# A time-mix block on one core: four result tiles in place of two, and six sequences laid out as four successive tokens a partition

## The chip, the core and the metric

The kernel runs on one core of one Trainium2 chip. The metric is the device time of one execution in microseconds. Three runs of the kernel before gave 110.7, 111.28 and 111.68 us, a median of 111.28 us.

## The reference, cut to what matters

The input `x` holds 8 sequences of 512 tokens with 128 channels, in float32. Everything is computed per token, save a recurrence along the tokens of a sequence.

```python
xn = layernorm(x)                                    # over the 128 channels
shifted = xn one token later                         # zero for the first token
k = (xn*mk + shifted*(1-mk)) @ Wk                    # v and r likewise, r through a sigmoid
rwkv = scan over tokens(time_decay, time_first, k, v)  # needs the tokens in order
s = (r * rwkv) @ Wo
h = relu(xn @ w1[0] + b1[0]);  eo = h @ w2[0] + b2[0]  # 128 -> 512 -> 128, expert 0 alone counts
g = silu(layernorm(xn + eo) * gamma + beta)
return x + s * g
```

## The kernel before, in words

A sequence `b` is one unit of work. Its 512 tokens are loaded as rows: `x_sb` holds, for each partition `p`, four blocks `j` of 128 channels. In the kernel before block `j` of partition `p` is token `j*128 + p`, so a partition's four tokens lie 128 tokens apart in memory, and a transfer moves 512 bytes at a time. Everything per row (the statistics of the layer norm, the normalised tile `xn`) works on these blocks. Then TensorE transposes the four 128x128 blocks of `xn` into one bank of PSUM (step `T`, L613), so that the partitions are channels and the 512 columns are the tokens in order. `xn` is the stationary operand there and the identity the moving one, and block `j` goes to columns `j*128` to `j*128+127`. ScalarE copies the bank to `xT` (L497). From there everything runs on tiles of 128 channels by 512 tokens: the mixed inputs `ink`, `inv`, `inr` (L786), the projections `k`, `v`, `r` (L630), the up projections `up0` to `up3` with their operand split into two float32r parts (L651 to L653), the down projections `z0` to `z3`, which accumulate onto the bank that `T` wrote (L680), the variance `var` (L668), the recurrence by three scans on VectorE, the gate, and the output projection `s` (L661). At the end `prod` = `s` times `g` is transposed back to rows (step `back`, L689: `prod` is stationary, block `j` is its columns `j*128` to `j*128+127`), VectorE adds the input rows and writes a tile `res` (step `res`, L875), and SyncE's queue stores it (L309).

Work on the eight sequences is interleaved. `PROGRAM` is a hand-written order of steps for each engine: `res:5` is step `res` of sequence 5, and `res.a:7` is the first half of it. Each step waits on semaphores for what it reads, and for the release of the buffer that it writes. Nearly every tile exists twice, and step `b` waits for the reader of step `b - 2`. Sequences 0 and 7 are worked in halves at the start and at the end: sequence 0's rows come in two transfers of 128 KB, sequence 7's results leave in two, `a` on SyncE's queue and `b` on ScalarE's.

With two result tiles, `res:b` waits until the store of sequence `b - 2` has landed (`stored`, L872). The queue of SyncE holds in this order: half of `x` of sequence 0, `w1`, the four square weights, `x` of sequence 1, `w2`, `x` of sequences 2 to 7, the stores of sequences 0 to 6, and `store.a:7`.

The end of VectorE's order is `res:3 prod:5 gated:7 res:4 zn.b:7 zn.a:7 prod:6 res:5 prod.a:7 prod.b:7 res:6 res.a:7 res.b:7`, that of TensorE's `back:3 s:5 var.b:7 var.a:7 back:4 s:6 s.b:7 back:5 s.a:7 back:6 back.a:7 back.b:7`.

Of the kernel before, what the change touches and what calls it, by code (L numbers as in the profile page):

```python
# [7 lines left out]
ALU = mybir.AluOpType  # L8
# [4 lines left out]
WARM_UP = 8  # L13
KEEP_WARM_BETWEEN = 1
KEEP_WARM = 4
LN_EXP_TABLES = "natural_log_exp_and_others"
SILU_TABLES = "silu_and_others"

# [110 lines left out]
def build_block(nc, x, vectors, squares, w1, w2, out):  # L129
    B, T, H = x.shape  # L130
    P = 128
    NT = T // P
# [1 line left out]
    NF = F // P  # L134
    assert H == P and T == 512 and NT * P == T and NF * P == F

    x_rows = x.rearrange("b (j p) c -> b p j c", p=P)
    out_rows = out.rearrange("b (j p) c -> b p j c", p=P)
    HALVES = [slice(0, NT // 2), slice(NT // 2, NT)]

    B1_COLUMN = len(VECTORS)
# [5 lines left out]
    with ExitStack() as ctx:  # L147
        def sb(name, *shape, dt=FP32):
            return ctx.enter_context(nc.sbuf_tensor(name, list(shape), dt))

        def pair(name, *shape, dt=FP32):
            return [sb(f"{name}_{n}", *shape, dt=dt) for n in range(2)]


        ident = sb("ident", P, P)
# [22 lines left out]
        ve1 = sb("ve1", P, B * NT)  # L178
        rstd1 = sb("rstd1", P, B * NT)
        xn = pair("xn", P, NT, P)  # L180
        res = pair("res", P, NT, P)


        xT = pair("xT", P, 1 + T)
# [26 lines left out]
        prod = pair("prod", P, T)  # L211
# [3 lines left out]
        def ps(name, b, half=""):  # L215
            return banks[bank_of[name, half if (name, half, b) in bank_of else "", b]]

        def sem(name):
            return ctx.enter_context(nc.semaphore(name))
# [5 lines left out]
                 "w2_sum", "w2_mean", "w2"]}  # L225
        done = {(engine, name): sem(f"{name}_by_{engine}")
                for engine, name in dict.fromkeys((signal[token][0], token[0]) for token in signal if token[2] is not None)}
        stored = [sem(f"stored_{n}") for n in range(2)]
        EDGES = 11
        LAST = B - 1  # L230
        CHUNKS = [f"z{f}" for f in range(NF)]

        def after(eng, step, b, half=""):
            if b < 0 or (b == 0 and step in NOT_FOR_FIRST):
                return
            if (step, half, b) in signal:
                engine, count = signal[step, half, b]
            elif half:
                engine, count = signal[step, "", b]
            else:  # L240
                engine, count = max(signal[step, h, b] for h in "ab")
            eng.wait_ge(done[engine, step], count)
# [4 lines left out]
        def bank_free(eng, name, b, half=""):  # L247

            previous = held_before[name, half, b]
            if previous == ("b2m", "", None):  # L250
                eng.wait_ge(prep["cols"], 4)
            elif previous:
                for step in FREED_BY[previous[0]]:
                    after(eng, step, previous[2], previous[1])

        def chunks_of(b):

            return [name for name, _, i in tokens("pe") if name in CHUNKS and i == b]
# [4 lines left out]
        def tiles(half):  # L263
            return {"": slice(0, NT), "a": HALVES[0], "b": HALVES[1]}[half]
# [8 lines left out]
        def first_on(engine, step):  # L273
            return [b for name, _, b in tokens(engine) if name == step][0]
# [23 lines left out]
        def load_half(eng, h):  # L298
            tiles = HALVES[h]
            eng.dma_start(x_sb[:, tiles.start * P:tiles.stop * P].rearrange("p (j c) -> p j c", c=P),  # L300
                          x_rows[0][:, tiles, :]).then_inc(got[f"x0_{h}"], 16)

        def load(eng, b):
            eng.dma_start(x_sb[:, b * T:(b + 1) * T].rearrange("p (j c) -> p j c", c=P),
                          x_rows[b]).then_inc(got[f"x{b}"], 16)

        def store(eng, b, half=""):
            after(eng, "res", b, half)
            eng.dma_start(out_rows[b][:, tiles(half), :], res[b % 2][:, tiles(half), :]).then_inc(stored[b % 2], 16)  # L309

        block = ctx.enter_context(nc.Block())

        @block.sync
        def _(sp):
            load_half(sp, 0)
            sp.dma_start(w1_in[:, :], w1).then_inc(got["w1"], 16)
            sp.dma_start(w_in[:, :, :], squares).then_inc(got["squares"], 16)
            load(sp, 1)
            sp.dma_start(w2_in[:, :, :], w2.rearrange("(f p) c -> p f c", p=P)).then_inc(got["w2"], 16)
            for b in range(2, B):  # L320
                load(sp, b)
            for b in range(LAST):
                store(sp, b)
            store(sp, LAST, "a")
            sp.wait_ge(stored[0], 16 * (B // 2))
            sp.wait_ge(stored[1], 16 * (B // 2 + 1))

        @block.gpsimd
        def _(pool):
# [117 lines left out]
        def _(act):  # L447
# [3 lines left out]
            def ln_exp_tables():  # L451
                act.preload_act_table_set(LN_EXP_TABLES)  # L452

# [137 lines left out]
            steps.update({f"hid{f}": hidden(f) for f in range(NF)})  # L591
            run("act", steps)
            store(act, LAST, "b")

        @block.tensor
        def _(pe):
            def keep_warm(count):
                for _ in range(count):
                    pe.matmul(banks[WARM_BANK][:, 0:P], ident[:, :], ident[:, :], start=True, stop=True)  # L599
# [8 lines left out]
            def transposes(b, half=""):  # L608
                if half != "b":
                    bank_free(pe, "z", b)  # L610
                after(pe, "norm1", b, half)
                for j in range(NT)[tiles(half)]:
                    ins = pe.matmul(ps("z", b)[:, j * P:(j + 1) * P], xn[b % 2][:, j, :], ident[:, :], start=j == 0,  # L613
                                    stop=False, is_transpose=True, skip_group_check=True)
                ins.then_inc(done["pe", "T"], 1)
                if half == "a":
                    keep_warm(KEEP_WARM_BETWEEN)
                elif b == 0:
                    keep_warm(KEEP_WARM)

# [63 lines left out]
            def back_to_rows(b, half=""):  # L684
                after(pe, "prod", b, half)
                bank_free(pe, "back", b, half)
                rows = ps("back", b, half)[:, :].rearrange("p (j c) -> p j c", c=P)
                for j in range(NT)[tiles(half)]:
                    ins = pe.transpose(rows[:, j, :], prod[b % 2][:, j * P:(j + 1) * P], ident[:, :])  # L689
                ins.then_inc(done["pe", "back"], 1)  # L690

            pe.wait_ge(prep["ident"], 1)
            keep_warm(WARM_UP)
            steps = {"b2m": b2_mean, "T": transposes, "var": variance, "s": project_out, "back": back_to_rows}
            steps.update({name: projection(name) for name in "kvr"})
            steps.update({f"up{f}": up(f) for f in range(NF)})
# [4 lines left out]
        def _(dve):  # L701
# [166 lines left out]
            def add_input(b, half=""):  # L868
                t = tiles(half)
                after(dve, "back", b, half)  # L870
                if b >= 2:
                    dve.wait_ge(stored[b % 2], 16 * (b // 2))  # L872
                rows = x_sb[:, b * T:(b + 1) * T].rearrange("p (j c) -> p j c", c=P)
                summed = ps("back", b, half)[:, :].rearrange("p (j c) -> p j c", c=P)
                dve.tensor_tensor(res[b % 2][:, t, :], summed[:, t, :], rows[:, t, :], ALU.add).then_inc(done["dve", "res"], 1)  # L875

            steps = {"bn": stats, "aggr1": aggregate, "norm1": normalise, "d": step_of_x, "xT_lo": low_part, "dv": value_steps,
                     "cols": small_columns, "w2_sum": w2_row_sums, "mx": running_max, "gap": exponents,
                     "den": denominator, "rel": relative, "dev": deviation,
                     "wkv": mixed_values, "gated": gate, "zn": scale, "prod": multiply, "res": add_input,  # L880
                     "adev": weighted}
            steps.update({"in" + name: mix(name) for name in "kvr"})
# [35 lines left out]
```

## Time and profile before

| | before |
|---|---|
| median of three runs | 111.28 us |
| the profiled execution | 111.6 us |
| its span, first to last instruction | 109.8 us |
| TensorE busy | 100.7 us, 92% |
| VectorE busy | 99.3 us, 90% |
| ScalarE busy | 93.4 us, 85% |
| GpSimd busy | 67.0 us, 61% |
| mean granted clock of TensorE | 0.986 |

The span leaves out 1.8 us of the profiled execution. Three engines are busy for 85% and more of the span, so which of them sets the pace at a given place is read from the chain of waits, followed back from the last instruction, and from the table of busy times by stretch. A matmul's busy time overlaps that of the next; the time that a matmul adds is read from the chain, where each piece counts once.

### The profile page before, as it was taken

To read this page: it belongs to the slowest core of one execution; us is meant where nothing else is said; L and a number is where in the kernel's file an instruction comes from. 1 tells how busy PE (TensorE), PEld (TensorE's weight loads), DVE (VectorE), ACT (ScalarE), POOL (GpSimd) and SP (SyncE) were. 2 spreads that over 40 slices of the span, in tenths; PEclk is the share of its full clock that TensorE was granted. 3 is DMA by queue.
4 is the path that set the end of the run, shared out by engine and by line. 5 is a ranking of instruction groups with operands and counts; after the bars stand their busy time and mean duration, and the time that the engine had idled before them with its cause. 6 is when DMAs were issued, how large, how long until landed. Compare 5 with 4: busy or idle time off the path is not lost.

```text
span 109.8 us, 1625 instructions
## 1 busy us (share of the span) xinstructions
PE 100.7 (92%) x340; PEld 57.8 (53%) x340; DVE 99.3 (90%) x204; ACT 93.4 (85%) x155; POOL 67.0 (61%) x102
## 2 busy tenths in 40 slices
PE   4999989999699999999999999999989999999720
PEld 4998546654346465436574554754424565435410
DVE  1789799999889999998999899999999999999941
ACT  3550888999979999999999999999998999998800
POOL 3059699986838599999699669594645033700000
PEclk9999999999999999999999999999999999999995
DMA  2999300000000000000005000000000020001463
GB/s 90 279 314 291 83 0 0 0 6 0 3 0 3 0 0 0 0 0 0 0 15 178 1 6 0 0 0 3 0 0 0 0 96 0 9 0 57 134 191 99
DMA packets 9450, 5.09 MB, mean 46 GB/s; under 512 B 480, under 2 KB 9184, under 8 KB 9440
## 3 DMA queue, kind: packets, MB, share of 16 engines
q1 hardware_dynamic: 8752, 4.72, 15.3%
q10 hardware_dynamic: 688, 0.27, 0.9%
q14 instruction: 7, 0.06, 0.2%
q8 instruction: 3, 0.05, 0.2%
HBM read 2.89 MB, written 2.10 MB: 45 GB/s over the span
## 4 chain that ended last, share of the span: by engine, by line
PE 56%; issue 15%; POOL 13%; ACT 6%; DVE 5%; DMA 2%; DVEq 1%; POOLq 0%; ACTq 0%
PE bank L630 11%; PE bank L680 10%; PE bank L599 5%; PE bank L661 5%; PE bank L668 5%; PE bank L651 4%; POOL xn L359 4%; PE bank L653 4%; PE bank L652 4%; PE bank L613 3%; PE bank L643 3%; POOL xT_lo L381 2%; DMA block_out<-res 2%; POOL gap_max L415 2%; PE bank L689 2%
## 5 line engine op out<-in xcount | busy, mean ns | idle before, releaser
L680 PE MATMUL bank<-hid,w_c 128*128 128x512 f32 x64 | 30.8, 593 | 0.3 <-ACT hid L514 0.3
L630 PE MATMUL bank<-mixed,w_in 128*128 128x512 f32 x48 | 24.0, 599 | 1.1 <-POOL mixed L399 1.1
L514 ACT ACTIVATE hid<-bank,vec 128x512 f32<-128x512 f32 x28 | 18.8, 684 | 3.6 <-PE bank L643 2.9
L680 PEld LDWEIGHTS bank<-hid,w_c 128*128 128x128 f32 x64 | 11.9, 189 | 12.6 <-issue 11.6
L786 DVE SCALAR_TENSOR_TENSOR mixed<-step_x,vec,bank 128x511 f32<-128x511 f32 x24 | 17.2, 735 | 0.8 <-POOL step_x L390 0.8
L651 PE MATMUL bank<-xT_hi,w_hi 128*128 128x512 f32 x28 | 15.7, 560 | 0.0
L359 POOL TENSOR_SCALAR xn<-x_sb,neg_mean,rstd 128x128 f32<-128x128 f32 x28 | 14.1, 521 | 0.1
L630 PEld LDWEIGHTS bank<-mixed,w_in 128*128 128x128 f32 x48 | 8.4, 189 | 9.3 <-issue 8.2
L423 POOL TENSOR_TENSOR dv<-v_sb 128x512 f32<-128x512 f32 x8 | 8.9, 1108 | 6.1 <-ACT v_sb L567 6.1
L825 DVE TENSOR_TENSOR_SCAN dev<-keep,dv 128x512 f32<-128x512 f32 x8 | 11.5, 1435 | 0.6 <-issue 0.3
L653 PE MATMUL bank<-xT_lo,w_hi 128*128 128x512 f32 x28 | 11.1, 395 | 0.0
L652 PE MATMUL bank<-xT_hi,w_lo 128*128 128x512 f32 x28 | 11.0, 394 | 0.0
L795 DVE TENSOR_TENSOR_SCAN mx<-td,bank 128x512 f32<-128x512 f32 x8 | 9.7, 1210 | 0.7 <-PE bank L630 0.7
L430 POOL TENSOR_SCALAR keep<-th_g 128x512 f32<-128x512 f32 x8 | 5.8, 723 | 6.3 <-ACT th_g L573 6.2
L810 DVE TENSOR_TENSOR_SCAN den<-e_keep,bank 128x512 f32<-128x512 f32 x8 | 9.6, 1208 | 0.0
L452 ACT ACT_TABLE_LOAD x6 | 7.7, 1283 | 1.9 <-issue 1.8
L710 DVE BATCH_NORM_STATS2 stats<-x_sb 128x6 f32<-128x128 f32 x32 | 6.9, 278 | 2.6 <-DMA x_sb<-x 2.6
L381 POOL TENSOR_TENSOR xT_lo<-xT,xT_hi 128x512 fp32r<-128x512 f32 x7 | 8.9, 1267 | 0.3
L668 PE MATMUL bank<-sq,averager 128*128 128x512 f32 (+1 forms) x18 | 8.3, 557 | 0.5 <-DVE adev L833 0.5
L661 PE MATMUL bank<-gated,wo_half 128*128 128x512 f32 (+1 forms) x18 | 8.3, 553 | 0.0
L651 PEld LDWEIGHTS bank<-xT_hi,w_hi 128*128 128x128 f32 x28 | 5.3, 188 | 5.5 <-issue 2.1
L407 POOL TENSOR_SCALAR gap_min<-gap,td 128x512 f32<-128x512 f32 x8 | 5.5, 688 | 4.2 <-DVE gap L803 4.0
(72 smaller groups left out, 209.9 us busy)
## 6 DMA issues: line engine op xcount, KB each, us to landing
x_sb<-x SPq DMA_DIRECT2D x7, 256.0 KB, 5.4
block_out<-res SPq DMA_DIRECT2D x7, 256.0 KB, 2.3
w_in<-w SPq DMA_DIRECT2D x2, 256.0 KB, 4.0
w_in<-squares SPq DMA_DIRECT2D x1, 256.0 KB, 3.9
x_sb<-x ACTq DMA_DIRECT2D x1, 128.0 KB, 2.8
x_sb<-x SPq DMA_DIRECT2D x1, 128.0 KB, 2.5
block_out<-res SPq DMA_DIRECT2D x1, 128.0 KB, 1.9
block_out<-res ACTq DMA_DIRECT2D x1, 128.0 KB, 2.0
```

The lines of the kernel that those rows point to most:

```text
L359: ins = pool.tensor_scalar(xn[n][:, j, :], x_tile(b, j), neg_mean1[:, i:i + 1], rstd1[:, i:i + 1], ALU.add, ALU.mult)
L381: pool.tensor_tensor(xT_lo[n][:, :], xT[n][:, 1:], xT_hi[n][:, :].bitcast(FP32), ALU.subtract).then_inc(done["pool", "xT_lo"], 1)
L514: act.activation(hid[b % 2][:, f, :], ps(f"up{f}", b)[:, :], ACT.Relu, bias=vec[:, B1_COLUMN + f:B1_COLUMN + f + 1]).then_inc(done["act", ...
L630: pe.matmul(ps(name, b)[:, :], w_in[:, which, :], mixed[b % 2][:, which, :], start=True, stop=True).then_inc(done["pe", name], 1)
L651: pe.matmul(dst, hi, xT_hi[n][:, :], start=True, stop=False)
L652: pe.matmul(dst, lo, xT_hi[n][:, :], start=False, stop=False)
L653: pe.matmul(dst, hi, xT_lo[n][:, :], start=False, stop=True).then_inc(done["pe", f"up{f}"], 1)
L661: pe.matmul(ps("s", b, half)[:, c], wo_half[:, :], gated[b % 2][:, c], start=True, stop=True).then_inc(done["pe", "s"], 1)
L668: pe.matmul(ps("var", b, half)[:, c], averager[:, :], sq[b % 2][:, c], start=True, stop=True).then_inc(done["pe", "var"], 1)
L680: pe.matmul(ps("z", b)[:, :], w2_c[:, f, :], hid[b % 2][:, f, :], start=False, stop=chunks_of(b)[-1] == f"z{f}", skip_group_check=True).th ...
L786: dve.scalar_tensor_tensor(mixed[n][:, which, 1:], step_x[n][:, 1:], vec[:, which:which + 1], ps("z", b)[:, 0:T - 1], ALU.mult, ALU.add).t ...
L825: dve.tensor_tensor_scan(dev[n][:, :], keep[n][:, 0:T], dv[n][:, :], 0.0, ALU.mult, ALU.add).then_inc(done["dve", "dev"], 1)
```

## The change

Two things change.

The result tile `res` exists four times (`RES = 4`), each with its own semaphore. `res:b` waits for the store of sequence `b - 4`, and SyncE waits at the end for four semaphores in place of two.

For sequences 1 to 6 partition `p` holds tokens `4p` to `4p+3` instead of `p`, `p+128`, `p+256`, `p+384`. A partition's four rows are then 2048 successive bytes in memory, for the load and for the store. So that the channel tiles still hold the tokens in order, `T` writes block `j` into every fourth column of the bank, from column `j` on, and `back` reads every fourth column of `prod` as its stationary operand. Sequences 0 and 7, worked in halves, keep the old layout. The number of transposes, their shapes and the bytes moved stay as they are.

```diff
+RES = 4
-    x_rows = x.rearrange("b (j p) c -> b p j c", p=P)
-    out_rows = out.rearrange("b (j p) c -> b p j c", p=P)
+    IN_HALVES = [0, B - 1]
+
+    def rows_of_tokens(a):
+        tiled, woven = a.rearrange("b (j p) c -> b p j c", p=P), a.rearrange("b (p j) c -> b p j c", j=NT)
+        return [tiled[b] if b in IN_HALVES else woven[b] for b in range(B)]
+
+    def columns_of(b, j):
+        return slice(j * P, (j + 1) * P) if b in IN_HALVES else slice(j, T, NT)
+
+    x_rows = rows_of_tokens(x)
+    out_rows = rows_of_tokens(out)
...
-        res = pair("res", P, NT, P)
+        res = [sb(f"res_{n}", P, NT, P) for n in range(RES)]
...
-        stored = [sem(f"stored_{n}") for n in range(2)]
+        stored = [sem(f"stored_{n}") for n in range(RES)]
...
-            eng.dma_start(out_rows[b][:, tiles(half), :], res[b % 2][:, tiles(half), :]).then_inc(stored[b % 2], 16)
+            eng.dma_start(out_rows[b][:, tiles(half), :], res[b % RES][:, tiles(half), :]).then_inc(stored[b % RES], 16)
...
-            sp.wait_ge(stored[0], 16 * (B // 2))
-            sp.wait_ge(stored[1], 16 * (B // 2 + 1))
+            for n in range(RES):
+                sp.wait_ge(stored[n], 16 * (B // RES + (n == LAST % RES)))
...
-                    ins = pe.matmul(ps("z", b)[:, j * P:(j + 1) * P], xn[b % 2][:, j, :], ident[:, :], start=j == 0,
+                    ins = pe.matmul(ps("z", b)[:, columns_of(b, j)], xn[b % 2][:, j, :], ident[:, :], start=j == 0,
                                     stop=False, is_transpose=True, skip_group_check=True)
...
-                    ins = pe.transpose(rows[:, j, :], prod[b % 2][:, j * P:(j + 1) * P], ident[:, :])
+                    ins = pe.transpose(rows[:, j, :], prod[b % 2][:, columns_of(b, j)], ident[:, :])
...
-                if b >= 2:
-                    dve.wait_ge(stored[b % 2], 16 * (b // 2))
+                if b >= RES:
+                    dve.wait_ge(stored[b % RES], 16 * (b // RES))
...
-                dve.tensor_tensor(res[b % 2][:, t, :], summed[:, t, :], rows[:, t, :], ALU.add).then_inc(done["dve", "res"], 1)
+                dve.tensor_tensor(res[b % RES][:, t, :], summed[:, t, :], rows[:, t, :], ALU.add).then_inc(done["dve", "res"], 1)
```

No instruction moves on any engine. What a step waits for changes at one place, VectorE's last steps, with the semaphores that each waits for (`stored_1` is that of result tile 1). Of the kernel before:

```order
L875 TENSOR_TENSOR res<-bank,x_sb 128x512 [waits stored_0,back_by_pe]
L858 SCALAR_TENSOR_TENSOR zn<-bank,cb,rstd_1 128x256 [waits silu_by_act,rstd2_by_act,sq_by_act] x2
L866 TENSOR_TENSOR prod<-bank,g 128x512 [waits back_by_pe,s_by_pe,silu_by_act]
L875 TENSOR_TENSOR res<-bank,x_sb 128x512 [waits stored_1,back_by_pe]
L866 TENSOR_TENSOR prod<-bank,g 128x256 [waits back_by_pe,s_by_pe,silu_by_act] x2
L875 TENSOR_TENSOR res<-bank,x_sb 128x512 [waits stored_0,back_by_pe]
L875 TENSOR_TENSOR res<-bank,x_sb 128x256 [waits stored_1,back_by_pe] x2
```

The same steps after the change:

```order
L885 TENSOR_TENSOR res<-bank,x_sb 128x512 [waits stored_0,back_by_pe]
L868 SCALAR_TENSOR_TENSOR zn<-bank,cb,rstd_1 128x256 [waits silu_by_act,rstd2_by_act,sq_by_act] x2
L876 TENSOR_TENSOR prod<-bank,g 128x512 [waits back_by_pe,s_by_pe,silu_by_act]
L885 TENSOR_TENSOR res<-bank,x_sb 128x512 [waits stored_1,back_by_pe]
L876 TENSOR_TENSOR prod<-bank,g 128x256 [waits back_by_pe,s_by_pe,silu_by_act] x2
L885 TENSOR_TENSOR res<-bank,x_sb 128x512 [waits stored_2,back_by_pe]
L885 TENSOR_TENSOR res<-bank,x_sb 128x256 [waits stored_3,back_by_pe] x2
```

The order is the same; the last two rows, `res:6` and the halves of `res:7`, wait for result tiles 2 and 3, that is for the stores of sequences 2 and 3, where they waited for those of 4 and 5.

## Rows read from the trace of the kernel before

**Rows 1.** The page: the chain that ended last, share of the span by engine.
```profile
PE 56%; issue 15%; POOL 13%; ACT 6%; DVE 5%; DMA 2%; DVEq 1%; POOLq 0%; ACTq 0%
```
**Rows 2.** Busy time by stretch: stretch and its length, then each engine's busy us.
```profile
42.00:55.00 13.00, 13.00 (x43) 6.81 (x43) 12.64 (x18) 12.84 (x22) 11.87 (x20) 1.00 0.00 0
55.00:66.00 11.00, 11.00 (x40) 6.11 (x39) 10.56 (x16) 10.97 (x19) 9.01 (x14) 1.00 0.16 50
98.00:105.00 7.00, 6.26 (x31) 3.63 (x28) 6.91 (x14) 5.48 (x9) 0.00 (x0) 1.00 0.27 85
```
**Rows 3.** The chain in order of time, its end: start us, us, what.
```profile
103.83 2.29 DMA block_out<-res
...
106.17 0.41 issue
106.58 0.06 DVE res L875
```
**Rows 4.** Instructions in order of time, VectorE and the last store: start us, us, engine, what.
```profile
100.06 7.35 SPq L309 DMA_DIRECT2D block_out<-res  x5
...
104.39 0.68 DVE L875 TENSOR_TENSOR res<-bank,x_sb 128x512 f32<-128x512 f32 x1
106.58 0.75 DVE L875 TENSOR_TENSOR res<-bank,x_sb 128x256 f32<-128x256 f32 x2 [1.52 <-DMA block_out<-res]
107.03 0.37 SPq L309 DMA_DIRECT2D block_out<-res  x1
107.37 0.40 ACTq L309 DMA_DIRECT2D block_out<-res  x1
```
**Rows 5.** Transposes back and a weight load before `s.b:7`, in order of time.
```profile
86.11 0.60 PE L689 MATMUL bank<-ident,prod 128*128 128x128 f32 x4
...
101.34 0.30 PEld L661 LDWEIGHTS bank<-gated,wo_half 128*128 128x128 f32 x2 [0.62 <-DVE gated L849]
...
103.35 0.63 PE L689 MATMUL bank<-ident,prod 128*128 128x128 f32 x4 [0.44 <-DVE prod L866]
104.28 0.74 PE L689 MATMUL bank<-ident,prod 128*128 128x128 f32 x4 [0.30 <-DVE prod L866]
```
**Rows 6.** Stretches at the end: the last column is GB/s, before it the DMA share.
```profile
106.00:106.95 0.95, 0.00 (x0) 0.00 (x0) 0.37 (x2) 0.00 (x0) 0.00 (x0) 0.83 0.90 272
107.03:107.90 0.87, 0.00 (x0) 0.00 (x0) 0.31 (x1) 0.00 (x0) 0.00 (x0) 0.50 0.03 9
107.90:108.87 0.97, 0.00 (x0) 0.00 (x0) 0.00 (x0) 0.00 (x0) 0.00 (x0) 0.50 0.87 266
```
**Rows 7.** The page's DMA issues: count, KB each, us to landing.
```profile
block_out<-res ACTq DMA_DIRECT2D x1, 128.0 KB, 2.0
```
**Rows 8.** Stationary loads of the transposes back: ns min/median/max, first and last start.
```profile
L689 PEld LDWEIGHTS bank<-ident,prod x32: 137/141/143, 54.6 to 104.6; 128*128 128x128 f32 x32
```
**Rows 9.** The chain in order of time: transposes, and a float32r matmul of 512 columns.
```profile
11.66 0.45 PE bank L613 x4
...
29.41 1.95 PE bank L630 x4
...
34.80 0.44 PE bank L613 x4
35.23 0.23 PE bank L651
...
57.03 0.44 PE bank L689 x4
...
75.28 0.87 PE bank L630 x2
```
**Rows 10.** Instructions in order of time around the loads of sequences 0 and 1.
```profile
6.61 0.87 DVE L710 BATCH_NORM_STATS2 stats<-x_sb 128x6 f32<-128x128 f32 x4 [0.49 <-DMA x_sb<-x]
...
6.99 0.66 ACT L497 ACTIVATE xT<-bank 128x256 f32<-128x256 f32 x2 [1.22 <-PE bank L613]
...
7.82 0.66 DVE L734 TENSOR_TENSOR step_x<-xT 128x512 f32<-128x512 f32 x1
```

## The prediction

> **What bounds the kernel now.** I read the chain of waits first, then the busy times by stretch, then the last 8 us in order of time. By share, the chain is 56% TensorE and 2% DMA [rows 1]. TensorE holds it without a break from 29.4 to 76.2 us [rows 9]: in those stretches it is busy for the whole length, 13.00 of 13.00 us and 11.00 of 11.00 us, with VectorE and ScalarE close behind [rows 2]. So in the middle each ns that a matmul adds is a ns of the kernel, while a transfer hides behind all of it. At the end VectorE takes over (6.91 of 7.00 us from 98 to 105 [rows 2]), and there stands the one thing that this change removes for certain: `res.a:7` waits 1.52 us for the store of sequence 5 [rows 4], which left at 103.83 and is on the chain for 2.29 us [rows 3].
>
> **Four result tiles.** `res:6` runs from 104.39 to 105.07, and `res.a:7` starts at 106.58 [rows 4]. With four tiles it waits for the store of sequence 3, issued at 100.06 [rows 4]. What is late next? Its transposes: `back.a:7` and `back.b:7` start at 104.28 and end at 105.02 [rows 5], so they are there. VectorE goes on at about 105.06, and both halves and both last stores come 1.5 us earlier: issues at about 105.5 and 105.85 in place of 107.03 and 107.37 [rows 4].
>
> Not all of the 1.5 us reaches the end, since the last bytes now meet those of sequence 6. Its store was issued at 105.09, and its bytes flow from 106.00 to 106.95 at 272 GB/s [rows 6]. The halves of 7 were issued at 107.03 and 107.37; nothing flows for 0.87 us, then both flow from 107.90 to 108.87 [rows 6], and the last lands at 107.37 + 2.0 = 109.37 [rows 4, 7], 0.5 us after its bytes. With the issue at 105.5 the 256 KB could flow from 106.4, but find the DMA engines at 0.90 share until 106.95 [rows 6]. So they flow from 106.95 to 107.92, in place of 108.87: **a gain of 0.95 us.** Were the last store free of what is ahead of it, it would land 2.0 us after 105.85, a gain of 1.5 us; that is the upper bound. The lower bound is 0.8 us: a late issue and two semaphores more to wait for, an estimate of 0.15 us, within the 0.41 us that VectorE took between the landing and its next start [rows 3]. I take 1.0, because longer rows for sequence 6 may shorten its flow a little.
>
> **Rows of 2048 bytes.** The loads and stores of six sequences move in a quarter of the pieces. Where could that be seen? Loads are waited for at one place behind the start: VectorE's statistics of sequence 1, 0.49 us [rows 10]. They end at 7.5, and what VectorE does next needs `xT` of sequence 0, which ScalarE finishes at 7.65, having waited itself for a transpose [rows 10]. At most 0.14 us of VectorE's time could come forward, and TensorE, which is on the chain there, doesn't wait for it. I count nothing. If the layout made transfers slower instead, that wait of 0.49 us is where it would show. In the stores only that of sequence 6 counts: its 0.95 us of flow could shrink by at most the 1.5 - 0.95 already in the bound.
>
> **Stepped transposes.** `T` of sequences 1 to 6 writes 24 blocks with a step of four columns, and `back` reads 24 stationary operands so. Nothing in the trace has such a pattern on TensorE, so both prices are bounded. Lower bound: 0 (no row gives a reason for a gain: same count, same columns). Upper bound: each takes twice its time. Four transposes add 0.44 us to the chain [rows 9], which is 0.86 ns a column. Doubled, a sequence's `T` costs 0.44 us more, and its `back` as much.
>
> Which is nearer? For the output there is a row: a float32r matmul puts 512 columns into a bank in 0.23 us [rows 9], 0.45 ns each. The bank can thus take columns at twice the pace of a transpose. If a stepped write costs the bank twice a neighbouring one, 0.9 ns, it stays just within the transposes' own 0.86 ns. I take 0 for `T`. For the stationary operand there is no such reserve in sight: a load takes 141 ns [rows 8] while the transposes follow each other every 110 ns [rows 9], so it is already as long as what hides it. I take 0 here too, with less confidence: it has a neighbour to hide behind, and only three of four loads in a group follow on another transpose's heels.
>
> **The sum.** 111.6 (the profiled execution) - 1.0 + 0 + 0 = 110.6. This execution was 0.3 us above the median of 111.28, so for a median **110.3 us**, 0.9% less.
>
> **The rivals.**
>
> *The stationary read is slow.* The load of every fourth column takes twice as long, so that a `back` takes 0.88 us in place of 0.44. Of six, that of sequence 1 stands in the full stretch at 57.03 [rows 9] and costs 0.44. That of sequence 2, at 86.11 us [rows 5], is between waits and costs 0 to 0.44. Those of 3 to 6 stand at the end, where TensorE has 0.62, 0.44 and 0.30 us of idle time before `s.b:7` and the last groups [rows 5]; four times 0.44 less what idle time absorbs before `res:6`, about 1.1, leaves 0.7. Sum 1.1 to 1.6, against a gain of 1.0: 111.4 to 111.9, say 111.6. Against it: the weight path works ahead of the matmuls (PEld is busy 6.11 of 11.00 us [rows 2]), so one load of four may be hidden. The Trainium skill, in "Advanced Engine Details and Errata", section Memory Cachelines, says that SBUF wants at least two accesses to a 16-byte line to hide its latency; a step of four float32 gives one, so by that rule this rival holds. No row shows it.
>
> *The stepped output is slow, and the kernel ends above the old time.* Mechanism: the bank takes a stepped column in twice the transpose's pace. Place: `T` of sequences 1, 3, 4, 5 and 6, which are on the chain (the first two are [rows 9]; that of 2 falls in a stretch where GpSimd holds the chain). Price: 5 x 0.44 = 2.2 us. With the 1.0 of the end: 111.28 + 1.2 = 112.5, slower by 1.1%. It decides from 50 ns a transpose on (20 x 50 ns = 1.0 us, the gain), and beyond 105 ns it is slower by over 1%. With the slow read as well, 113.6 to 114.1. Against it: the 0.45 ns a column [rows 9]. The same page and section of the Trainium skill says that PSUM has 8-byte lines and that "Any non-contiguous AP significantly slows down matmuls". By that sentence this rival wins; the trace has no stepped output, and so cannot confirm it. The row speaks for a reserve at the pace of a float32 transpose, and the rule names no pace, which is why I give it one chance in five and not more.
>
> *The gain at the end stays out.* Four tiles do what they say by their waits, but if the last bytes are held up by the two stores ahead more than reckoned, the 0.95 shrinks to some 0.3 us: 111.0. For it: the DMA engines are at 0.87 to 0.90 share in each burst [rows 6]. Against it: bursts of 256 KB took 0.95 and 0.97 us, without exception in what I read.
>
> **How the numbers follow.** Forecast (no price for the step, 0.8 to 1.5 us gained) 0.50, its own range 109.6 to 110.6; slow read 0.20; slow output, with or without the slow read, 0.20; the gain stays out 0.10. Less than 1%, some 1.1 us, can hardly be told from no change here. The forecast's gain lies on that line: 0.9% expected, 1.3% at the upper bound. I give 0.32 of the 0.50 to faster, as the long rows can only add to the gain of sequence 6's store. The other 0.18, the slow read but for 0.03, the missing gain and 0.04 of the slow output (50 to 100 ns a transpose) are within 1%: 0.18 + 0.17 + 0.10 + 0.04 = 0.49. Slower: 0.16 + 0.03 = 0.19. The range from 109.5 to 112.6 leaves out the double price (0.1) and what is unforeseen on the good side.
>
> **What would show it.** In the profile of the changed kernel: VectorE's last `res` rows follow `res:6` with no wait; the last store's issue near 105.8 and its landing 2.2 to 2.5 us later, by the queue ahead. Four stepped transposes as pieces of 0.44 us on the chain mean no price; 0.88 at L623 is the slow output, 0.88 at L699 with loads above 141 ns the slow read. Packets on SyncE's queue fewer by 12 x 384. I would be wrong if the transposes lengthen, or if the whole program, busy on three engines, falls into other waits in the middle.

## The result, and the profile after

The changed kernel took 110.18 us (median of 6 runs, 110.08 to 110.74), the kernel before 111.31 us beside it: a ratio of 0.9908, 95% interval 0.9881 to 0.9935. A second series (12 runs, e4 below) gave 0.9933, interval 0.9910 to 0.9956. The change is worth 0.7 to 0.9%. The ratios leave out the few executions that took over 1.5% longer than the fastest of the same kernel; the profile of e6 is of one of these (131.59 us, mean granted clock 0.761).

The profiled execution took 110.08 us, its span is 108.2 us, 1.6 us less than the 109.8 of before (1.52 by the traces' 109.77 and 108.25). That is more than the medians differ by, and where it comes from has to be asked by parts. First the end, instructions in order of time (start us, us, engine, what), the answer to [rows 4]:

```profile
98.58 0.68 DVE L885 TENSOR_TENSOR res<-bank,x_sb 128x512 f32<-128x512 f32 x1
...
103.62 1.35 DVE L885 TENSOR_TENSOR res<-bank,x_sb 128x512 f32<-128x512 f32 x3
105.00 0.40 ACTq L319 DMA_DIRECT2D block_out<-res  x1
```

`res:6`, `res.a:7` and `res.b:7` are now one unbroken group of 1.35 us. The wait of 1.52 us is gone. From the start of `res:6` to the issue of the last store it took 107.37 - 104.39 = 2.98 us before and takes 105.00 - 103.62 = 1.38 now: 1.6 us less, where 1.5 was forecast. But the page's issues say when the stores land (KB each, us to landing), the answer to [rows 7]:

```profile
block_out<-res SPq DMA_DIRECT2D x7, 256.0 KB, 2.0
...
block_out<-res SPq DMA_DIRECT2D x1, 128.0 KB, 2.4
block_out<-res ACTq DMA_DIRECT2D x1, 128.0 KB, 2.8
```

The last store lands 2.8 us after its issue in place of 2.0, and gives 0.8 back. The end gains 1.6 - 0.8 = 0.8 us (0.74 by the spans to the hundredth). The rest, 0.8 us, stood already at `res:3`: 98.58 here, 99.36 before. It arises at the start, where TensorE and the load of sequence 1 meet:

```profile
6.24 0.38 PE L623 MATMUL bank<-ident,xn 128*128 128x128 f32 x2
6.72 0.66 ACT L507 ACTIVATE xT<-bank 128x256 f32<-128x256 f32 x2 [0.98 <-PE bank L623]
6.77 0.87 DVE L720 BATCH_NORM_STATS2 stats<-x_sb 128x6 f32<-128x128 f32 x4 [0.68 <-DMA x_sb<-x]
7.35 3.62 PE L653 MATMUL bank<-xT,w_in 128*128 128x256 f32 x16
...
10.81 0.60 PE L623 MATMUL bank<-ident,xn 128*128 128x128 f32 x4
```

The up projections start at 7.35. In the kernel before:

```profile
6.26 0.63 PE L613 MATMUL bank<-ident,xn 128*128 128x128 f32 x2
...
6.68 1.51 PE L599 MATMUL bank<-ident 128*128 128x128 f32 x8
8.04 3.62 PE L643 MATMUL bank<-xT,w_in 128*128 128x256 f32 x16
...
11.50 0.60 PE L613 MATMUL bank<-ident,xn 128*128 128x128 f32 x4
```

They start at 8.04: two transposes last 0.63 us in place of 0.38, and the eight matmuls on the identity that keep TensorE at work 1.51 in place of 1.06. This is TensorE's clock. The views print a granted clock of 1.00 for both stretches, but they do so also where the trace holds no record of it, and its records begin only later: at 7.64 us before and at 6.22 in the changed kernel, both at full clock. A matmul on the identity takes 421 ns ahead of that moment and 275 behind it (ns min/median/max; the first line is the kernel before, 6.6 to 7.4 us, the second the changed one, 6.4 to 7.4):

```profile
L599 PE MATMUL bank<-ident x4: 421/421/421, 6.7 to 7.3; 128*128 128x128 f32 x4
L609 PE MATMUL bank<-ident x9: 275/275/368, 6.0 to 7.2; 128*128 128x128 f32 x9
```

From one to the next it is 0.21 us ahead of it and 0.11 behind it, so TensorE ran at the lower of its two clocks, 1.2 GHz, for 7.64 - 6.22 = 1.42 us longer before the change. At half the pace that loses 0.71 us, and the up projections start 0.69 us apart. Is that the change or chance? e4, the same program, tells it.

Of the stepped columns, the lines of the transposes (ns min/median/max), the answer to [rows 8]:

```profile
L623 PE MATMUL bank<-ident,xn x32: 272/273/454, 5.4 to 69.7; 128*128 128x128 f32 x32
L699 PEld LDWEIGHTS bank<-ident,prod x32: 137/197/220, 53.8 to 103.9; 128*128 128x128 f32 x32
L699 PE MATMUL bank<-ident,prod x32: 270/283/358, 54.2 to 104.0; 128*128 128x128 f32 x32
```

The stepped output costs nothing: the transposes of `T` have a median of 273 ns. The stepped operand does cost something, 197 ns a load in place of 141. On the chain the groups of four weigh what they did in [rows 9], or 0.03 us more:

```profile
34.10 0.44 PE bank L623 x4
...
54.31 0.44 PE bank L699 x4
56.31 0.47 PE bank L699 x4
```

(54.31 is sequence 0, without a step; 56.31 is sequence 1, with it.) And the loads, in a stretch with the changed kernel's engine times, then granted clock, DMA share and GB/s; the first row is the changed kernel's:

```profile
7.00:9.80 2.80, 2.80 (x17) 2.50 (x16) 2.77 (x11) 1.08 (x5) 1.62 (x5) 1.00 1.04 379
```

and the same stretch before:

```profile
7.00:9.80 2.80, 2.80 (x17) 2.58 (x17) 2.77 (x11) 1.35 (x5) 1.82 (x5) 1.00 1.22 292
```

With rows of 2048 bytes in `x` this stretch moves 379 GB/s, with rows of 512 bytes 292. In the first, 94% of the bytes go in packets of 2048, in the second all in packets of 512. It is the same for the stores: in full flow one moves 360 GB/s (101.9 to 102.6 us), before it was 277 (102.75 to 103.65).

### The profile page after: what moved, and what is told of

Same layout as the page of the kernel before. It is cut to its first block, busy times and chain, and to the rows that moved or that the text cites. A ratio compares the mean times of both kernels' runs of the same rounds, so it can differ in the third digit from the quotient of the medians.

```text
span 108.2 us, 1624 instructions
## 1 busy us (share of the span) xinstructions
PE 100.1 (92%) x340; PEld 57.9 (54%) x340; DVE 99.2 (92%) x204; ACT 93.3 (86%) x155; POOL 66.8 (62%) x102
## 3 DMA queue, kind: packets, MB, share of 16 engines
q1 hardware_dynamic: 4144, 4.72, 12.7%
## 4 chain that ended last, share of the span: by engine, by line
PE 56%; issue 15%; POOL 13%; ACT 6%; DVE 5%; DVEq 0%; POOLq 0%; ACTq 0%
PE bank L640 12%; PE bank L690 10%; PE bank L671 5%; PE bank L678 5%; PE bank L609 5%; PE bank L661 4%; POOL xn L369 4%; PE bank L663 4%; PE bank L662 4%; PE bank L623 3%; PE bank L653 3%; POOL xT_lo L391 2%; POOL gap_max L425 2%; PE bank L699 2%; DVE dev L835 2%
```

## The experiments

Each run is compared with runs of the kernel before on the same chip. "Faster by" is one minus the ratio, with the 95% interval of the ratio.

**e1: four result tiles alone.**

```diff
-    IN_HALVES = [0, B - 1]
+    IN_HALVES = list(range(B))
```

> The change's first half alone: four result tiles, all eight sequences in the old layout. Theory (the tail carries the gain): the wait of 1.52 us before res.a:7 is gone, the last two stores are issued 1.5 us earlier after res:6 than before, but wait for the bytes of sequence 6; net 0.8 to 1.0 us, so 110.3 to 110.5 us, all of the change's gain or nearly. Rival (the long rows carry it, by shortening loads and stores): less than 0.4 us gained, 110.9 or more.

Measured 110.90 us beside 111.39, ratio 0.9950 (0.9928 to 0.9972): 0.5% or 0.55 us faster. The forecast of 110.3 to 110.5 missed: the gain is more than half of the change, but less than the theory's 0.8 to 1.0, and lies only a little above the rival's limit of 0.4. Its stores show why (us to landing):

```profile
block_out<-res SPq DMA_DIRECT2D x1, 128.0 KB, 2.6
block_out<-res ACTq DMA_DIRECT2D x1, 128.0 KB, 3.1
```

3.1 us, 0.3 more than in the changed kernel and 1.1 more than before. From 108.2 us on, the queues of the two stores still move this (GB/s in 40 slices to 109.5 us, then packets by queue):

```profile
GB/s 16 16 32 16 16 32 16 32 16 16 0 0 0 0 0 0 0 0 0 0 0 0 0 0 0 0 0 0 0 0 0 0 0 0 0 0 0 0 0 0
DMA packets 15, 0.01 MB, mean 5 GB/s; under 512 B 2, under 2 KB 15, under 8 KB 15
```

15 packets, 13 of them of 512 bytes, trickle at 16 to 32 GB/s for 0.3 us. The trickle began at 108.06, where the full flow ends (stretch and its length, engine times, granted clock, DMA share, GB/s):

```profile
106.10:108.06 1.96, 0.00 (x0) 0.00 (x0) 0.00 (x0) 0.00 (x0) 0.00 (x0) 1.00 0.87 262
108.06:108.54 0.48, 0.00 (x0) 0.00 (x0) 0.00 (x0) 0.00 (x0) 0.00 (x0) 1.00 0.08 21
```

With all 16 engines at work the same queues move some 290 GB/s, so 21 is about the rate of one. And the packets of 512 bytes start one at a time from 108.06 on, 0.023 us apart, from the two queues in turn. The trace doesn't name the engines, but this is what one engine would leave that lags behind the others, and the store ends when it does. The changed kernel has the same trickle in its last stretch, 106.9 to 108.2 us:

```profile
GB/s 32 16 16 32 16 32 16 16 32 16 16 0 0 0 0 0 0 0 0 0 0 0 0 0 0 0 0 0 0 0 0 0 0 0 0 0 0 0 0 0
DMA packets 18, 0.01 MB, mean 6 GB/s; under 512 B 3, under 2 KB 18, under 8 KB 18
```

The kernel before does not have it; its last bytes break off within some 0.1 us (108.5 to 109.8 us):

```profile
GB/s 268 284 331 284 252 299 299 268 315 237 189 142 48 16 0 0 0 0 0 0 0 0 0 0 0 0 0 0 0 0 0 0 0 0 0 0 0 0 0 0
```

**e2: the long rows and the stepped transposes alone.**

```diff
-RES = 4
+RES = 2
```

> The change's second half alone: rows of 2048 bytes and the stepped transposes, two result tiles. Theory: res.a:7 still waits for the store of sequence 5, but that store now lands about 0.3 us earlier (its flow at some 380 GB/s in place of 290), so the wait is 1.2 us in place of 1.5; 110.9 to 111.2 us in all. Rival (the long rows carry the gain): 110.3 or less. Rival (the stepped transposes cost something): 111.4 or more.

Measured 111.18 us, ratio 0.9976 (0.9955 to 0.9997): 0.27 us faster by the ratio, as the theory said, though the interval reaches to 0.03%. The wait is still there, shorter by the 0.3 us that the store of sequence 5 needs less (it lands after 2.0 us in place of 2.3):

```profile
106.36 0.75 DVE L885 TENSOR_TENSOR res<-bank,x_sb 128x256 f32<-128x256 f32 x2 [1.23 <-DMA block_out<-res]
```

The two halves of the change add up within their intervals: 0.50% + 0.24% against the 0.67% of e4.

**e3: the columns left as they were.** The long rows stay, so the tokens are not in order and the recurrence is not the reference's; the same instructions run.

```diff
-        return slice(j * P, (j + 1) * P) if b in IN_HALVES else slice(j, T, NT)
+        return slice(j * P, (j + 1) * P)
```

> The changed kernel with its long rows, but the transposes write and read neighbouring columns as before; this leaves out putting the tokens in order. Theory (steps are nearly free): the stationary loads of the transposes back return from 197 to 141 ns, and the kernel gains 0.0 to 0.2 us against the changed one, 110.0 to 110.2 us. Rival (slow stationary read costs something that the gain hides): 0.3 us or more faster than the changed kernel, 109.9 or less.

Measured 110.85 us, ratio 0.9946 (0.9923 to 0.9969), beside e4's 110.75. The forecast of 110.0 to 110.2 missed, as e4's own did. Without steps the kernel is not faster than e4, and the stationary loads were back at 138/140/142 ns. The two medians alone can't tell 0.3 us, but the profiles can: from the second `xT` to the end it is 97.05 us without steps and 97.07 with them (table below). The rival is out.

**e4: the change again.**

> The changed kernel again, beside the others on one chip. 110.2 us within 0.3. What tells something is the start: in the profile of the kernel before, the matmuls on the identity after the first transposes took 1.51 us for eight, in that of the changed one 1.06 us, and all that follows stands 0.7 us earlier. If that is chance, the start of the up projections (8.04 before, 7.35 changed) varies from profile to profile between those values, for every kernel; if the change makes it, it is near 7.35 in each profile with long rows and near 8.04 in the run with the old layout.

Measured 110.75 us, ratio 0.9933 (0.9910 to 0.9956), 0.25 us above the range expected; its interval overlaps that of the first series. Its start is what it was run for:

```profile
7.17 3.62 PE L653 MATMUL bank<-xT,w_in 128*128 128x256 f32 x16
7.46 0.87 DVE L720 BATCH_NORM_STATS2 stats<-x_sb 128x6 f32<-128x128 f32 x4 [1.28 <-DMA x_sb<-x]
...
11.33 0.66 PE L623 MATMUL bank<-ident,xn 128*128 128x128 f32 x4 [0.54 <-POOL xn L369]
```

The up projections start even earlier than in the first profile, at 7.17, but the second group of transposes only at 11.33: it waits for `xn` of sequence 1, and that for a load which landed at 7.44. The start of the up projections follows neither branch of the expectation: 7.69 with the old layout (e1), 7.99 with the long rows (e2). So two things race at the start, TensorE's early matmuls, by the moment at which its clock rises, and the landing of sequence 1, and both vary from run to run. In e1 the statistics of sequence 1 started at 7.58, in e2 at 7.45, in e3 at 7.99, before at 6.61: no order by layout. The 0.7 us of the first pair of profiles is mostly luck. The races end at the second `xT`; by it the span divides into three parts:

| profile | clock recorded from | start, to the second `xT` | middle, to `res:3` | end |
|---|---|---|---|---|
| before | 7.64 | 12.13 | 87.23 | 10.44 |
| changed | 6.22 | 11.45 | 87.13 | 9.62 |
| e1, four tiles alone | 6.90 | 12.14 | 87.38 | 9.98 |
| e2, long rows alone | 7.45 | 12.09 | 87.33 | 10.18 |
| e3, changed without steps | 6.05 | 12.55 | 87.39 | 9.66 |
| e4, changed again | 4.71 | 12.03 | 87.40 | 9.67 |
| e7, rows of 1024 bytes too | 7.71 | 12.18 | 87.21 | 10.01 |
| e8, sequence 1 loaded first | 5.62 | 11.44 | 87.13 | 9.63 |
| e9, the same again | 4.67 | 11.71 | 87.25 | 9.54 |
| e12, before, sequence 1 first | 5.16 | 11.05 | 87.26 | 10.39 |

(Start: when `xT` of sequence 1 starts, L497 or L507 with 128x512. End: from the start of `res:3` to the span's end, e1: 109.5 - 99.52 = 9.98; as spans are given to 0.1 us, it is good to 0.05.) In each profile TensorE's matmuls shorten from 421 to 275 ns within 0.3 us of the moment in the second column. The middle is 87.1 to 87.4 us with steps or without. The end is the change's doing: 10.44 to 9.62 and 9.67, of which e1 brings 0.46 and e2 0.26.

**e5: the price of a step by itself.** Behind TensorE's last step:

```diff
+            for _ in range(16):
+                pe.transpose(scratch[:, 0:P], x_sb[:, 0:P], ident[:, :])
+            for _ in range(16):
+                pe.transpose(scratch[:, 0:T:NT], x_sb[:, 0:P], ident[:, :])
...
+            for _ in range(16):
+                pe.transpose(scratch[:, 0:P], x_sb[:, 0:T:NT], ident[:, :])
...
+            for _ in range(16):
+                pe.matmul(scratch[:, 0:2 * P:2], id16[:, 0:P], id16[:, 0:P], start=True, stop=True)
```

> The changed kernel with nine groups of matmuls appended on TensorE behind its last step, on a bank that nothing reads any more: 8 on the identity, then 16 each of a float32 transpose with neighbouring output and operand; output step 4; operand step 2; operand step 4; operand step 8; then a bf16 matmul of 128 columns with output step 1, 2 and 4. Theory (the bank has a reserve at a float32 transpose's pace): output step 4 leaves the transposes at 0.11 us apart, operand steps lengthen the stationary load to 197 ns at step 4 and the spacing by no more than 0.03 us; for bf16, whose columns come at twice the pace, the stepped output costs up to twice. Rival (any step slows the write): output step 4 puts the float32 transposes 0.15 us apart or more. Rival (steps never cost): bf16 keeps its spacing at step 2 and 4.

Instructions in order of time, one row for each group of 16:

```profile
106.72 1.91 PE L717 MATMUL bank<-ident,x_sb 128*128 128x128 f32 x16
...
108.46 1.91 PE L719 MATMUL bank<-ident,x_sb 128*128 128x128 f32 x16
...
110.21 2.08 PE L721 MATMUL bank<-ident,x_sb 128*128 128x128 f32 x16
...
112.12 2.09 PE L723 MATMUL bank<-ident,x_sb 128*128 128x128 f32 x16
...
114.05 1.98 PE L725 MATMUL bank<-ident,x_sb 128*128 128x128 f32 x16
...
115.86 1.06 PE L727 MATMUL bank<-ident 128*128 128x128 bf16 x16
...
116.75 1.91 PE L729 MATMUL bank<-ident 128*128 128x128 bf16 x16
...
118.46 1.95 PE L731 MATMUL bank<-ident 128*128 128x128 bf16 x16
```

This is one execution. The start of the next group less the start of one, by 16, is the spacing. Plain transposes (L717): 109 ns. Output step 4 (L719): 1.75 / 16 = 109 ns, no price. Operand step 2, 4 and 8 (L721, L723, L725): 119, 121 and 113 ns, with stationary loads of 208, 209 and 196 ns in place of 141. Then bf16, whose columns come at twice the pace: 56 ns with neighbouring output (L727), 107 ns with output step 2 (L729), and step 4 (L731) lasts as long. So here a stepped output costs nothing where a column comes every 0.85 ns, and twice the time where one comes every 0.43. Both halves of the theory hold, and both rivals fall.

**e6: without the store of sequence 6.** Its rows of the output are left out.

```diff
-            for b in range(LAST):
+            for b in range(LAST - 1):
                 store(sp, b)
```

> The changed kernel without the store of sequence 6, whose rows of the output are left out. Theory (the last stores queue behind it): the store of the last half, which lands 2.8 us after its issue in the changed kernel, lands after 2.0 us as before the change, and the run is 0.7 to 0.9 us shorter than the changed one. Rival (the 2.8 us come from two stores issued close together): the landing stays at 2.4 or more and the gain below 0.4 us.

The last half landed after 2.1 us, so the 2.8 come from what is ahead, as the theory said. (This run takes away the bytes ahead and the trickle together, and doesn't tell one from the other.) The time was 109.99 us beside 111.19, ratio 0.9885 (0.9851 to 0.9918), 0.25 to 0.5 us less than the change's own ratios of 0.9908 and 0.9933: short of the 0.7 to 0.9 expected and partly within the rival's "below 0.4". The landing speaks for the theory's cause; its size is not settled by the three runs that the ratio rests on.

**e7: rows of 1024 bytes for sequences 0 and 7.** Two successive tokens a partition within each half; the load and the store of a half index these rows.

```diff
+        pairs, woven = a.rearrange("b (h p i) c -> b p h i c", h=2, i=2), a.rearrange("b (p j) c -> b p j c", j=NT)
+        return [pairs[b] if b in IN_HALVES else woven[b] for b in range(B)]
...
+        return slice(j // 2 * 2 * P + j % 2, (j // 2 + 1) * 2 * P, 2) if b in IN_HALVES else slice(j, T, NT)
```

> The changed kernel with sequences 0 and 7 laid out too: within each half, two successive tokens a partition (rows of 1024 bytes), transposed with every second column. Theory (short rows cost the last stores part of their time): the bytes of the last two stores flow at 330 GB/s or more in place of 290, 0.1 to 0.3 us less at the end, and the first load lands 0.1 us earlier; 0.1 to 0.4 us faster than the changed kernel. Rival (the end hangs on one DMA engine that lags): under 0.1 us.

Measured 110.58 us, ratio 0.9951 (0.9930 to 0.9971): no gain over the change, rather a loss. The bytes did flow faster, 350 GB/s from 106.0 to 107.3 us, but the last store landed after 3.1 us, behind a trickle of 0.8 us at 19 to 37 GB/s. That is what the rival says: at the end it is the slowest engine that counts, not the rate of all.

**e8 and e9: sequence 1 loaded before the square weights.** This came out of e4.

```diff
-            sp.dma_start(w_in[:, :, :], squares).then_inc(got["squares"], 16)
             load(sp, 1)
+            sp.dma_start(w_in[:, :, :], squares).then_inc(got["squares"], 16)
```

> The changed kernel with the load of sequence 1 issued ahead of the four square weights on SyncE's queue. Theory (in about half the runs the start hangs on the landing of sequence 1, whose statistics started between 6.6 and 8.0 us in six profiles): the statistics start near 6.1, the second group of transposes follows the up projections without a wait, and the median falls by 0.2 to 0.5 us. Rival (the start hangs on TensorE's matmuls alone): no change within 0.1 us.

> The changed kernel with the load of sequence 1 ahead of the square weights, once more, beside the three others on one chip. If its gain is real: 0.9% to 1.2% below the kernel before, and the second group of transposes starts within 0.1 us of the end of the up projections, with no wait for GpSimd.

e8: 110.02 us, ratio 0.9898 (0.9869 to 0.9927); e9: 110.27 us, ratio 0.9907 (0.9873 to 0.9941). In both profiles the second group of transposes follows the up projections with no wait: 3.46 us from the start of one to that of the other, as before (11.50 - 8.04):

```profile
6.28 0.87 DVE L720 BATCH_NORM_STATS2 stats<-x_sb 128x6 f32<-128x128 f32 x4
...
7.34 3.62 PE L653 MATMUL bank<-xT,w_in 128*128 128x256 f32 x16
...
10.80 0.60 PE L623 MATMUL bank<-ident,xn 128*128 128x128 f32 x4
```

e9 kept only the lower end of its forecast, and its interval includes both of the change's own ratios. Sequence 1 is no longer waited for, so what is left at the start is the clock: in the profiles of e8 to e12 it rose at 4.67 to 5.62 us, earlier than in all others but e4. These profiles therefore flatter the start, and the size of the gain is read from the medians alone.

**e10 and e11: the last stores.** Both on top of e8. e10 has one store of 256 KB for sequence 7, e11 has both halves on SyncE's queue.

```diff
-            store(sp, LAST, "a")
+            store(sp, LAST)
...
-            store(act, LAST, "b")
```

```diff
             store(sp, LAST, "a")
+            store(sp, LAST, "b")
...
-            store(act, LAST, "b")
```

> As e9, with one store of 256 KB for sequence 7 in place of two halves. Theory (the last bytes wait for those of sequence 6 and for one DMA engine that lags): the later issue of the first half costs nothing; the same time within 0.2 us, or up to 0.3 us less. Rival (issuing early matters): 0.3 us more.

> As e9, with both halves of sequence 7 stored from SyncE's queue. Theory (the lag is that of one DMA engine, which fetches instructions meanwhile, whatever the queue): a trickle of 16 to 33 GB/s still ends the transfers, and the time is that of e9 within 0.2 us. Rival (the lag comes from two queues taking turns): the trickle is gone, the last landing falls from 2.7 to 2.3 us or less, and the kernel gains 0.3 us.

e10: 109.95 us beside 111.52, ratio 0.9880 (0.9843 to 0.9916), the fastest of all and 1.2% below the kernel before; e11: 110.01 us, ratio 0.9883 (0.9851 to 0.9915). Neither can be told from e9 or from the other. No worth of the first half's early issue can be seen, as expected. e11 still has a trickle of some 20 GB/s for 0.4 us after its last burst, and the later of its halves lands after 2.6 us, not 2.3 or less, so two queues taking turns are not the cause of the lag.

**e12: sequence 1 first in the kernel before.** The edit of e8, on the kernel before.

> The kernel before with that one edit, the load of sequence 1 ahead of the square weights; rows of 512 bytes and two result tiles. Theory (the landing of sequence 1 bounds the start in either layout): 0.2 to 0.5 us faster than before, and with the change's 0.8 us this makes up e9. Rival (only the faster loads of the long rows profit): within 0.1 us of before.

Measured 110.87 us, ratio 0.9942 (0.9920 to 0.9963): 0.65 us faster, more than expected. With the 0.75 of e4 this would make 1.4 us, 110.1; e8 and e9 lie at 110.0 and 110.3. The table agrees that the start and the end are separate gains: e12 has the end of the kernel before (10.39 against 10.44), e8 that of the changed one.

## Why the prediction was right, point by point

**The place.** The chain of waits was rightly read: the one removable wait stood at `res.a:7` [rows 3, 4], it is gone, and the middle did not move (87.1 to 87.4 us in all profiles of the table). SyncE's queue has 8752 - 4144 = 4608 packets fewer, the 12 x 384 forecast.

**The 1.5 us at the issue of the last store** are 1.6 in the profile.

**Four tiles, 0.95 us of gain.** This term was too large, and another's absence made up for it. Alone, four tiles shorten the end by 0.46 us (e1). The reasoning that the bytes of sequence 7 queue behind those of 6 was right, and e6 supports it: without that store the landing falls from 2.8 to 2.1 us. Counted from the start of `res:6`, the prediction has the last bytes at 107.92 - 104.39 = 3.53 us, and the full flow of e1 ends at 108.06 - 104.56 = 3.50. What it missed is the trickle behind that, 0.48 us in e1, which neither burst of 256 KB in [rows 6] shows; it makes up nearly all of the 0.5 us by which the 0.95 fell short. So the sign that was named, a landing 2.2 to 2.5 us after the issue, came out at 2.8 in the changed kernel.

**Rows of 2048 bytes, next to nothing.** This term was too small: 0.26 us at the end (e2), where the step from 0.95 to 1.0 had allowed 0.05. I had let the shorter flow of sequence 6 enter as "a little", since no row told rates by row length apart. In the profile after they are apart, 379 against 292 GB/s on the loads. At the start they gave nothing, as said, though for another reason than I gave. I wrote that TensorE doesn't wait for the load of sequence 1; in the profile that I had, this was true by 1.1 us (`xn` of sequence 1 was done at 10.43, its transposes started at 11.50), and in e1, e3 and e4 TensorE does wait. One profile shows one margin, not its spread.

**Stepped output, nothing.** Right, and for the reason given, the reserve at the pace of a float32 transpose. e5 shows a pace at which it costs: at bf16's, half the time a column, the same step doubles the time. The sentence of the Trainium skill, "Any non-contiguous AP significantly slows down matmuls" ("Advanced Engine Details and Errata", section Memory Cachelines), is confirmed for bf16 (56 to 107 ns) and does not hold for the float32 transpose (109 and 109 ns).

**Stepped operand, nothing.** Right in sum, not in size: the load takes 197 ns, 1.4 times and not twice, and a transpose comes 12 ns later at step 4 (e5), 0.03 us a group on the chain; e3 against e4 shows nothing in the total. The Trainium skill's rule, in the same page and section, of two accesses to a 16-byte line would let step 2 go free and charge step 4; measured, step 2 costs as much as 4 (119 and 121 ns).

**The sum** of the two mis-sized terms, 0.46 + 0.26, is 0.7 us, and the end gained 0.7 to 0.8, against the 1.0 forecast: one term too large and one too small, which is luck in the number and not in the place. That the time of 110.18 fell so close to 110.3 may owe something to luck at the start too: e4's 110.75 is the same program, and its ratio makes a gain of 0.75 us. Of the rivals, neither step had a price on the chain beyond 0.03 us a group. The third, that the last bytes are held up by the stores ahead more than reckoned, came half true: e1's gain shrank from 0.95 to 0.46 us, nearer to its 0.3, and only the long rows brought the sum back.

## What to carry to other kernels

When a buffer wait at the end of a kernel goes, price the last transfer by what is queued ahead of it on the DMA engines, and by the slowest of them, not from the issue alone; the 1.6 us earlier issue was worth 0.8. A float32 transpose can lay tokens out with a step for free, at 0.85 ns a column here, so that transfers can have long rows; a bf16 matmul at 0.43 ns a column can't. And compare starts over several profiles before crediting a change with them: here two races moved the start by 0.6 us with the same program (11.45 and 12.03), and the moment at which TensorE's clock rises was one of them.

## What was not expected of the hardware

The last bytes of a burst can trickle for 0.3 to 0.8 us at 16 to 37 GB/s, as if one of the 16 DMA engines were late. It was seen in all profiles in which the stores of 6 and 7 run into one another (changed, e1, e3, e4, e5, e7, e8 to e11) and in none of those where a gap lies between them (before, e2, e6, e12). In the first group a fetch of instructions, one packet of some 8 KB, falls into or just ahead of the flow; in the second it falls into the gap. That would explain the lag, 8 KB at one engine's 20 GB/s being 0.4 us: the packets that trickle come to 6 to 10 KB in all of these but e7. In e7 it is some 19 KB, more than twice what the fetch would leave. No run moved the fetch, so it stays an argument. Open too is why TensorE's clock rises at 4.67 us in one run and at 7.71 in another, though its first matmul starts at 1.5 us in each.
